# Third layer's low-rank factor kept in SBUF, adapters picked on TensorE, a bias folded into the weights, and the passage to the third layer reordered

## The reference, cut to what matters

```python
# dense 1: a weight masked in 32 x 32 blocks
out = x @ (W0 * block_mask).T
# dense 2: a weight, a bias, and one adapter of rank 16 chosen for each batch
y = x @ W1.T + bias
seg = searchsorted(starts, arange(B), side='right') - 1
adapter = clip(seg - 1, 0, 2)            # three adapters
y += where(seg > 0, (x @ A[adapter].T) @ B[adapter].T, 0)
# the attention-like layer: 1024 -> 128, four sub-layers (scan over tokens, MLP), 128 -> 1024
h = x @ Win.T + bin
for l in range(4):
    h = h + sconv(silu(layernorm(h) * ln1_w + ln1_b)) * sc_lin
    h = h + mlp(layernorm(h) * ln2_w + ln2_b)
out = (layernorm(h) * lnl_w + lnl_b) @ Wout.T + bout
# dense 3: a weight, a bias and eight experts of rank 16, mixed for each batch by a router
q = x[:, 179:-1].mean(axis=1)
routing = softmax(q @ router_W.T + router_b)
out = x @ W.T + b + 2 * sum_e routing_e * (x @ A_e.T) @ B_e.T
```

## Time and profile before

| | |
|---|---|
| median of 3 runs | 1789.1 us (1788.26 to 1795.86) |
| the profiled execution | 1785.82 us, span 1784.1 us, mean granted clock 0.978 |
| PE / weight loads | 1707.3 us (96%) / 1373.2 us (77%) |
| DVE / ACT / POOL | 1068.6 us (60%) / 654.7 us (37%) / 441.0 us (25%) |
| DMA | 199.76 MB, 112 GB/s; queues q1 and q10 (hardware dynamic), q8 and q14 (instructions) |
| dense 1, about | 0 to 375 us |
| dense 2, about | 375 to 880 us |
| MLP turns, about | 880 to 1244 us |
| passage and first pair | 1244 to 1320 us |
| dense 3, about | 1320 to 1784 us |

### The profile page before, as it was taken

How to read it: one execution, slowest core, us unless ns; L and a number is a source line. 1 busy time by engine, 2 the same in 40 slices (tenths; PEclk the granted TensorE clock), 3 DMA queues, 4 the chain that set the end, 5 groups by cost and what they waited for, 6 DMA issues and landing times.

```text
span 1784.1 us, 23303 instructions
## 1 busy us (share of the span) xinstructions
PE 1707.3 (96%) x8154; PEld 1373.2 (77%) x8154; DVE 1068.6 (60%) x2045; ACT 654.7 (37%) x967; POOL 441.0 (25%) x380
## 2 busy tenths in 40 slices
PE   6999999999999999999799999999699899999998
PEld 5788888888888888888666676666578688787886
DVE  6433443445555555566667777778567676776633
ACT  2433333333333333322334555545333333433321
POOL 4011111100000000000466777763122221211200
PEclk9999999999999999999889999999799999999999
DMA  6323333333323333333040000003445555555321
GB/s 249 107 94 119 115 122 121 122 112 116 112 102 114 109 108 110 109 114 107 39 151 24 1 1 1 1 15 124 155 131 213 162 191 186 178 181 183 126 94 60
DMA packets 81541, 199.76 MB, mean 112 GB/s; under 512 B 9746, under 2 KB 26130, under 8 KB 81170
## 3 DMA queue, kind: packets, MB, share of 16 engines
q1 hardware_dynamic: 60690, 129.07, 21.8%
q10 hardware_dynamic: 20736, 69.22, 9.7%
HBM read 125.89 MB, written 72.35 MB: 111 GB/s over the span
## 4 chain that ended last, share of the span: by engine, by line
PE 88%; DVE 4%; issue 4%; ACT 2%; POOL 1%; DMA 1%; ACTq 0%; SPq 0%; POOLq 0%; DVEq 0%
PE ps L666 19%; PE ps L668 18%; PE ps L667 18%; PE ps L843 6%; PE ps L788 3%; PE ps L680 3%; PE ps L725 2%; PE ps L794 2%; PE ps L834 2%; PE ps L835 2%; PE ps L833 2%; PE ps L727 2%; PE ps L726 2%; PE ps L749 1%; PE ps L811 1%
## 5 line engine op out<-in xcount | busy, mean ns | idle before, releaser
L666 PE MATMUL ps<-wall_x,x_hi 128*128 128x512 f32 x1008 | 399.8, 397 | 7.7 <-DVE wall_x L1328 3.7
L668 PE MATMUL ps<-wall_x,x_lo 128*128 128x512 f32 x1008 | 395.0, 392 | 0.0
L667 PE MATMUL ps<-wall_x,x_hi 128*128 128x512 f32 x1008 | 394.8, 392 | 0.0
L1926 POOL TENSOR_TENSOR rstd<-var_eps,minus_half 128x1 f32<-128x1 f32 x96 | 78.0, 812 | 925.1 <-DVE minus_mean L1363 917.9
L1354 DVE BATCH_NORM_STATS2 stats<-row 128x6 f32<-128x512 f32 x192 | 133.0, 694 | 183.1 <-ACT row L1038 178.8
L666 PEld LDWEIGHTS ps<-wall_x,x_hi 128*128 128x128 f32 x1008 | 190.6, 189 | 50.7 <-issue 10.3
L668 PEld LDWEIGHTS ps<-wall_x,x_lo 128*128 128x128 f32 x1008 | 190.6, 189 | 40.8
L667 PEld LDWEIGHTS ps<-wall_x,x_hi 128*128 128x128 f32 x1008 | 190.9, 189 | 37.9
L666 PE MATMUL ps<-wall_y,x_hi 128*128 128x512 f32 x512 | 202.8, 396 | 0.0
L668 PE MATMUL ps<-wall_y,x_lo 128*128 128x512 f32 x512 | 200.1, 391 | 0.0
L667 PE MATMUL ps<-wall_y,x_hi 128*128 128x512 f32 x512 | 199.7, 390 | 0.0
(11 more groups left out here) (243 smaller groups left out, 2935.9 us busy)
## 6 DMA issues: line engine op xcount, KB each, us to landing
x_scratch<-row ACTq DMA_DIRECT2D x64, 512.0 KB, 2.9
x_in<-x_scratch SPq DMA_DIRECT2D x64, 512.0 KB, 3.6
w_in<-in_w_t SPq DMA_DIRECT2D x96, 256.0 KB, 2.9
out<-row ACTq DMA_DIRECT2D x32, 512.0 KB, 2.6
x_in<-in_x_t SPq DMA_DIRECT2D x29, 512.0 KB, 3.4
cx<-x_scratch SPq DMA_DIRECT2D x24, 512.0 KB, 3.9
x_scratch<-cx ACTq DMA_DIRECT2D x24, 512.0 KB, 2.7
w_more<-in_w_t SPq DMA_DIRECT2D x32, 256.0 KB, 3.0
```

What stands on the lines that cost most here:

```text
L666: pe.matmul(bank, hi[:, k], wall[:, k, 0, cols], start=(k == 0), stop=False)
L667: pe.matmul(bank, hi[:, k], wall[:, k, 1, cols], start=False, stop=False)
L668: return pe.matmul(bank, lo[:, k], wall[:, k, 0, cols], start=False, stop=(k == KC - 1))
L1926: pool.tensor_tensor(rstd[:, i:i + 1], var_eps[:, i:i + 1], minus_half[:, 0:1], ALU.pow)\
```

## The change

1. Dense 2. The factors of all adapters are loaded once, 64 rows twice (the second copy in partitions 64 to 127), and `lora_hi` and `lora_low` make of them one fp32r matrix with the high parts in the first 64 rows and the low parts, with a sign, in the others. `choose(b)` scales a placement matrix by `coef`, and PE picks with it: `pick_b` gives the batch's B (2 matmuls of 512 columns), `pick_a` the chunk of A (1 matmul of 128 columns for every two parts); ACT copies both from PSUM (`take_b`, `take_a`). High and low parts lie in different rows of one operand, so a part is one matmul in place of three.
2. Dense 3. `expert_a` is loaded and split once, in dense 1, and stays in SBUF (`a_hi`, `a_lo`, 8 KB for each partition). The room comes from the descriptor reserve, 16 KB before and 1 KB now (`dynamic_dma_scratch_size=1024`, `CONST`).
3. The bias of the read-out. z is taken plus one (`one`, the bias of `silu_x`), the bias row over 128 is added to every row of `wout`, and the fourth matmul, `brow`, `ones`, `two_ones` and `bias_low` go.
4. The passage. The loop ends at turn 37; what was left is written out in another order. `rstd1` and `var1` are double, and units 38 and 39 have their own banks (`s1_bank`). LAG is 6.
5. Semaphores of the statistics are folded into `dve_done`.

```diff
-LAG = 4
+LAG = 6
-TURNS = LAST_END + 1
+TURNS = MLP_END + 6
...
-    CONST = 16512
+    CONST = 1152
...
     def weight_part(n):
...
-                pe.wait_ge(a_hi_ready, n // 2 + 1)
-                pe.wait_ge(a_lo_ready, n // 2 + 1)
+                if n < BATCHES * PARTS:
+                    pe.wait_ge(a_rows_ready, n // 2 + 1)
                 if n % PARTS == 0:
                     pe.wait_ge(b_hi_ready, 2 * b + 2)
-                    pe.wait_ge(b_lo_ready, 2 * b + 2)
+                bank = ps[:, part_bank(n)]
                 if n < BATCHES * PARTS:
                     at_least(pe, w_summed, n)
+                    pe.matmul(bank, a_rows[:, i], b_rows[:, cols], start=True, stop=True).then_inc(w_product, 1)
+                    return
...
+            def pick_b(b, half):
+                if half == 0:
+                    pe.wait_ge(pick_ready, b + 1)
+                    pe.wait_ge(lora_ready, 2)
+                    at_least(pe, w_summed, PARTS * b)
                 else:
+                    pe.wait_ge(b_hi_ready, 2 * b + 1)
+                pe.matmul(ps[:, 4], pick[:, 1], lora[:, 1, half * HALF:(half + 1) * HALF], start=True, stop=True)\
+                  .then_inc(b_picked, 1)
+
+            def pick_a(chunk):
+                k, i = chunk % KC, chunk % 2
+                at_least(pe, a_rows_ready, chunk - 1)
+                at_least(pe, h_evacuated, (chunk - KC - 2) // 2)
+                pe.matmul(ps[:, 7, HALF // 2 + P * i:HALF // 2 + P * (i + 1)], pick[:, 0], lora[:, 0, k * P:(k + 1) * P],
+                          start=True, stop=True).then_inc(a_picked, 1)
...
-                    pe.matmul(bank, lo, wout_hi[:, cols], start=False, stop=False)
-                    pe.matmul(bank, ones_rows[:], brow[:, cols], start=False, stop=True).then_inc(c_mm, 1)
+                    pe.matmul(bank, lo, wout_hi[:, cols], start=False, stop=True).then_inc(c_mm, 1)
...
             for s in range(A_END, B_END):
                 b, j, i = batch_of(s), s % TPB, s - A_END
+                if b + 1 < BATCHES and j == 0:
+                    pick_b(b + 1, 0)
+                if b + 1 < BATCHES:
+                    pick_a(KC * (b + 1) + j)
                 if s + 1 < B_END:
                     turn_x(s + 1)
-                product(s, 0)
+                if b + 1 < BATCHES and j == 0:
+                    product(s, 0, range(KC // 2))
+                    pick_b(b + 1, 1)
+                    product(s, 0, range(KC // 2, KC))
+                else:
+                    product(s, 0)
...
-                if turn == 37:
-                    turn_x(B_END)
-                if turn == 38:
-                    read_out(TPB)
-                if turn == 39:
-                    reduce_total(0)
+            turn_x(B_END)
+            spread_rstd1(LAST_END - 3)
+            variance1(LAST_END - 2)
+            variance1(LAST_END - 1)
+            read_out(TPB)
+            spread_rstd1(LAST_END - 2)
+            spread_rstd1(LAST_END - 1)
+            reduce_total(0)
             router_logits(0)
+            router_turn(0)
             read_out(TPB + 1)
-            router_turn(0)
...
# ACT, passage
+            square1(LAST_END - 2)
+            normalise_c(TPB - 2)
+            square1(LAST_END - 1)
+            silu_x(LAST_END - 3)
+            normalise_c(TPB - 1)
+            split_x(B_END)
+            silu_x(LAST_END - 2)
             router_exp(0)
             split_b(BATCHES)
-            normalise_c(TPB)
...
+                    silu_x(LAST_END - 1)
+                    build_parts(n, range(2))
                     split_x(p + 1)
-                    build_parts(n, range(PARTS))
+                    build_parts(n, range(2, 4))
+                    normalise_c(c)
+                    build_parts(n, range(4, PARTS))
...
# DVE, start of the MLP and passage
                     scale_wout()
-                    two_ones()
                 if turn == EARLY + 6:
-                    bias_low()
                     wout_low()
...
+            take_var1(LAST_END - 2)
+            take_var1(LAST_END - 1)
+            add_up(TPB - 2, 0)
+            scale1(LAST_END - 3)
+            add_up(TPB - 1, 0)
+            add_up(TPB - 1, 1)
+            scale1(LAST_END - 2)
+            split_x(B_END)
+            take_q(0)
+            residual_half(TPB, 0)
             router_first(0)
-            split_a(BATCHES * PARTS // 2)
             router_second(0)
+            residual_half(TPB, 1)
             take_coef(0)
+            residual_end(TPB)
             split_b(BATCHES)
...
+                    scale1(LAST_END - 1)
+                    build_parts(n, range(2))
                     split_x(p + 1)
-                    build_parts(n, range(2))
-                    residual(c + 1)
-                    build_parts(n, range(2, PARTS))
+                    build_parts(n, range(2, 3))
+                    residual_half(c + 1, 0)
+                    build_parts(n, range(3, 4))
+                    residual_half(c + 1, 1)
+                    residual_end(c + 1)
+                    build_parts(n, range(4, PARTS))
...
# SP, passage
-            for m in range(3, UNITS):
+            for m in range(3, UNITS - 2):
                 store_z(m)
             load_x(B_END + 1)
+            for i in range(2, 4):
+                load_w(BATCHES * PARTS + i)
+            for m in range(UNITS - 2, UNITS):
+                store_z(m)
...
# POOL, turns and passage
+                for c in first_tiles(turn - 1)[1:]:
+                    root_c(c)
                 for c in first_tiles(turn - 2):
                     add_up(c)
-                for c in first_tiles(turn - 1)[1:]:
-                    root_c(c)
-                if turn == 39:
-                    root_c(TPB)
+            root1(LAST_END - 2)
+            root1(LAST_END - 1)
+            add_up(TPB - 2)
+            root_c(TPB)
```

More of the change, by code:

```diff
@@ new lines, in weight_part @@
+                    return
+                if n % PARTS == 0:
+                    pe.wait_ge(a_lo_ready, 1)
+                    pe.wait_ge(b_lo_ready, 2 * (b - BATCHES) + 2)
+                pe.wait_ge(w_summed, n - 1)
+                rows = slice(k * P, (k + 1) * P)
+                pe.matmul(bank, a_hi[:, rows], b_hi[:, cols], start=True, stop=False)
+                pe.matmul(bank, a_hi[:, rows], b_lo[:, cols], start=False, stop=False)
+                pe.matmul(bank, a_lo[:, rows], b_hi[:, cols], start=False, stop=True).then_inc(w_product, 1)
@@ L915, in _ @@
                     turn_x(A_END)
+                if s >= PARTS and s % 2 == 0:
+                    pick_a((s - PARTS) // 2)
                 product(s, 0)
+                if s == PARTS - 1:
+                    pick_b(0, 0)
                 if s >= PARTS:
@@ L1415, in adapter_coef @@
                 dve.wait_ge(small_loaded, 7 * 16)
-                dve.wait_ge(adapter_parts, 2)
-                after(dve.memset(coef[:], 0.0))
+                dve.wait_ge(ident_ready, 1)
+                for i, first in enumerate((0, LOW)):
+                    rows = ident[:, first:first + ADAPTERS * RANK]
+                    mark(dve.tensor_reduce(group[:, i], rows.rearrange("p (a j) -> p a j", j=RANK), AX, ALU.add))
                 for b in range(BATCHES):
-                    after(dve.tensor_scalar(below[:, b], starts[:], float(b), None, ALU.is_le))
+                    mark(dve.tensor_scalar(below[:, b], starts[:], float(b), None, ALU.is_le))
@@ L1420, in adapter_coef @@
+                settle()
+                mark(dve.tensor_tensor(group[:, 0], group[:, 0], group[:, 1], ALU.add))
                 after(dve.tensor_reduce(count[:], below[:], AX, ALU.add))
[L1421 to L1423 removed]
+                for i in range(ADAPTERS):
+                    mark(dve.tensor_scalar(chosen[:, i], count[:], float(i + 2), None, ALU.is_equal))
@@ new lines, in adapter_coef, with pick_places @@
+                settle()
+                after(dve.tensor_scalar(coef[:, 0:BATCHES], chosen[:, 0], group[:, 0, 0:1], None, ALU.mult))
+                for i in range(1, ADAPTERS):
+                    after(dve.scalar_tensor_tensor(coef[:, 0:BATCHES], chosen[:, i], group[:, 0, i:i + 1],
+                                                   coef[:, 0:BATCHES], ALU.mult, ALU.add))
+            def pick_places():
+                mark(dve.memset(low_row[:], 0.0))
+                after(dve.memset(place[:], 0.0))
+                mark(dve.memset(low_row[LOW:], 1.0))
+                for i in range(2):
+                    for g, first in enumerate(((0, 0, LOW), (0, LOW, 0))[i]):
+                        rows = ident[:, first:first + ADAPTERS * RANK]
+                        mark(dve.tensor_reduce(place[:, i, RANK * g:RANK * (g + 1)],
+                                               rows.rearrange("p (a j) -> p j a", j=RANK), AX, ALU.add))
+                settle()
+                after(dve.tensor_scalar(row_sign[:], low_row[:], -2.0, 1.0, ALU.mult, ALU.add))
@@ L1425, in take_biases, with choose, lora_low @@
```

(7 more changed lines are left out.)

307 lines of the change are left out of this document (157 added, 150 removed).

## The result

The changed kernel took 1727.61 us (median of 4 runs, 1726.88 to 1728.08); the kernel before took 1788.68 us beside it. The ratio is 0.965, with a 95% interval of 0.9624 to 0.9675: 61 us faster. The forecast was 1720 us, the range 1704 to 1741. The sum of the terms was 67.5 us; the two profiled executions differ by 58.4 us (1784.1 and 1725.7 us of span), less than the medians, since that of the kernel before (1785.82 us) was 2.9 us under its median.

A forecast was written before the change was run, and what follows sets the result against it. TensorE (PE), busy 96% of the span, was taken as the bound. Terms of 23.0, 12.7, 3.5, 10.7 and 17.6 us sum to 67.5, giving 1718.3 from the profiled execution and 1721.6 from the median; forecast 1720 us, range 1704 to 1741.

The forecast's parts named there:

- A: Dense 2 weight parts: one matmul instead of three, less the picks, plus waits gone at batch starts; net gain 23.0 us.
- I take 0.2: Dense 2: assumed PE time in us for each of 32 pick_a matmuls, 6.4 us in all, because a lone matmul pipelines badly.
- The lower end: Dense 2: pick_a's cost from below, by 256-column starts 0.12 us apart and 128-column transposes at 0.109 us; total 3.5 us.
- Rival 1: Dense 2: picks stall PE, which waits for ACT's copies; 1803 us at 2.6 us more per tile; chance 2%.
- B: Read-out in MLP turns and dense 3: bias matmul folded away, 60 x 0.2267 = 13.6 us, less tile 7's four: 12.7 us.
- C: Start of the MLP: bias_low and other bias work go, so PE's wait for z and half the half-clock loss go; 3.5 us.
- What bounds: Opening section: TensorE busy 96% of the span; a removed wait of another engine counts only if PE stood behind it.
- Rival 3: Dense 3 read-out tiles: DVE becomes the bound and the 44 folded matmuls give nothing; 1730 us; chance 8%.
- D: Passage from the MLP to dense 3: new order brings the first parts sooner; gain 10.7 us, four bias matmuls included.
- Rival 2: Passage stays as long as it was, first parts at half clock, only four matmuls gained; 1730 us; chance 15%.
- E: Dense 3 weight builds: resident A removes first-part waits and half clock for second to fourth batch (6.0, 4.8, 6.8); 17.6 us.

The follow-up runs named there:

- first experiment: Changed kernel with GpSimd's order in the MLP turns undone, its two add_up again before the root of the odd tile: 1724.07 us, 3.5 us less.

## Why the prediction came out as it did

The sum was 67.5 us and the executions gave 58.4; what was off, step by step:

- **A** (23.0, measured 26.8). The 29.0 us for the matmuls stand (30.5 when put back). The step that failed is "I take 0.2" for pick_a: 32 x 0.07 = 2.2 us, not 6.4, 4.2 us less, which accounts for the difference of 3.8. The lower end was made from the right rows; the argument that a lone matmul between two kinds pipelines badly is what the runs refute. The Trainium skill's 81 ns (TensorE: Matmul & The Clock Gate, "Back-to-back issue gap") lies near the lone pick's 0.07 us and under the 0.112 us of the further ones. Rival 1 never showed: PE waited for no pick.
- **A low clock at tile 60** (-1.5, no term). It is under "The hardware" below.
- **B in the MLP and C** (6.2, measured 0.5). I priced the folded matmuls at full PE and VectorE's work by its durations in the kernel before. GpSimd's new order was followed only in the passage, and I never asked what it would run beside. The step that failed is that VectorE's operations were taken at a fixed duration: GpSimd over VectorE took back 3.3 us (first experiment), and wout_lo takes 2.32 us over GpSimd's rotation. Another 0.9 us went at the start of the MLP (27.3 us at half clock from 851.42 on, 23.9 before). That is not the change: the unaltered kernel has 23.9 us there in its second trace, and does not lose them. With C's 0.7 us below, 0.8 us of the 5.7 are left, less than the 1.5 us of the folded matmuls that the test with the fourth matmul finds hidden. C was forecast at 3.5 us; 2.8 of it shows between the two kernels, in the turn where bias_low stood, and put back it costs 5.3, of which 3.0 in the profiled execution is in the passage.
- **B in dense 3** (10.0, measured 5.6). "What bounds": the cover checked was VectorE, and it held, 11.95 us of 14.49. What became late was x_in, and PE's load of x was priced at no wait without a look at its queue: SyncE's was read for the passage only. Rival 3 named the right tiles and the wrong engine; 4.4 of its 10 us came true, 2.9 of them by SyncE's order.
- **D** (10.7, measured 10.1). PE's timeline in the passage after, against the earlier trace rows:

```profile
1228.51 1.92 PE L921 MATMUL ps<-token_weight,total 128*128 128x1 f32 x16 [1.53 <-DVE total L1811]
1231.71 0.55 PE L928 MATMUL ps<-rw,q 128*1 128x8 f32 x16 [1.28 <-DVE q L1819]
1234.64 0.26 PE L933 MATMUL ps<-ident,wide 1*128 1x1 f32 x1 [2.39 <-DVE wide L1832]
1238.52 0.76 PE L743 MATMUL ps<-b_hi,a_hi 128*128 128x512 f32 x1 [0.76 <-DVE b_lo L1457]
```

  From turn_x(B_END) to the first part it is 20.0 us; the prediction had 20.1 (27.2 before). From there to the pair's end it is 45.0; the prediction had 44.5. The chain laid out for VectorE came true step by step: coef ends 17.5 us after turn_x(B_END) (17.6 in the prediction), b_lo 19.8 (20.0), and weight sum 4 ends 14.7 us after the first part (14.7). That the size is right owes a little to errors that cancel: LAG 6 cost 1.4 us against the 1 us allowed for a low clock, and the steps named from the low part at 1280.6 on add up to about 1307.1, not 1307.7. Half clock lasted 17.06 us in the two stretches shown next, but they end before weight sum 2 (1246.34), while PE was behind VectorE's chain; that they cost nearly nothing is read from the timelines and was not run. Of these 10.1 us, resident factors alone give 2.1. What each move in the order gives was not run.

```profile
1223.47:1226.88 3.41, 3.02 (x11) 1.73 (x9) 1.85 (x4) 2.15 (x3) 3.41 (x3) 0.50 0.00 0
1230.30:1243.95 13.65, 9.22 (x42) 7.05 (x42) 10.45 (x26) 4.28 (x8) 0.56 (x1) 0.50 0.45 158
```

  Rival 2 was right that half clock stays, and wrong that the length stays: the first parts do run at half clock, but the chain ahead of them is VectorE's and not PE's.
- **E** (17.6, measured 17.2, and 17.2 alone). 4.9, 5.3 and 6.9 us stand against 6.0, 4.8 and 6.8. The clock followed the wait: no idle ahead of the first part, no half clock in these tiles.

## What to carry to other kernels

When a tile on the bound engine gets shorter, check every queue that feeds it at the new length, the DMA issuer's before the vector engine's: the next wait here was a load that stood in order behind another one's wait. When an order is changed on GpSimd or VectorE, lay the two timelines side by side: here a VectorE operation with both inputs in SBUF ended only after the GpSimd operation that it met, and one taken out of VectorE's list handed its wait on to the next. Before a difference of a microsecond is given a cause, read a second trace of the same kernel: here one stage differed by 0.8 us with nothing changed. Price a matmul that a trace lacks from the start-to-start distance of the same number of columns, not from a guess about changes of kind.

## What the runs showed of the hardware

- VectorE and GpSimd. The two sums of each engine in the MLP of the changed kernel, one instruction to a line:

```profile
1206.83 1.28 POOL L2110 TENSOR_TENSOR total<-c_first,total 128x512 f32<-128x512 f32 x1
1206.87 1.79 DVE L1814 TENSOR_TENSOR total<-c_first,total 128x512 f32<-128x512 f32 x1
1208.26 1.54 POOL L2110 TENSOR_TENSOR total<-c_first,total 128x512 f32<-128x512 f32 x1
1208.77 1.58 DVE L1814 TENSOR_TENSOR total<-c_first,total 128x512 f32<-128x512 f32 x1
```

  VectorE's sum takes 0.69 us where GpSimd does not read beside it. Here each ends 0.55 us after GpSimd's (1208.66 after 1208.11, 1210.35 after 1209.80), and GpSimd's second, which starts inside VectorE's first, takes 1.54 us and not 1.28. wout_lo (1.22 us alone) ends 1.08 us after the rotation's end at 934.83, and bias_low in the kernel before 1.08 us after its end at 959.22. In the changed kernel's trace all 31 of VectorE's sums and differences of 512 columns with both inputs in SBUF that start during a 512-column operation of GpSimd end 0.55 to 0.58 us after it. Operations with an input in PSUM keep 0.68 us. So the later one waits until the other has ended, for all but 0.14 us of itself, and the lost time is what is left of the other's operation. The Trainium skill ("SBUF — State Buffer", section "Who interferes with whom") says that a VectorE instruction with two SBUF inputs contends with a GpSimd instruction that reads SBUF, calls the shared ports an exclusive lock and has the order of issue decide who blocks. These rows agree: one after the other, the four would take 1.28 + 0.69 + 1.27 + 0.69 = 3.93 us, and with 0.14 us less at each of the three changes 3.51; they took 3.52.
- The clock can fall with no idle time ahead of it. At tile 60 the changed kernel has this stretch, 0.9 us after 32 matmuls of one column, with PE busy all the time:

```profile
761.57 3.62 PE L814 MATMUL ps<-vec,w 128*128 128x1 f32 x32
```

```profile
766.09:769.50 3.41, 3.41 (x10) 2.64 (x9) 2.17 (x3) 1.54 (x2) 0.32 (x1) 0.50 0.19 73
```

  The kernel before and the one with the parts three times run the same 32 matmuls in 3.6 us and stay at full clock. With five picks the stretch is 6.82 us; with only the resident factors added to the kernel before it is 3.41 us again. Since that kernel's dense 2 is the one of the kernel before, and the kernel before has one trace, the -1.5 us cannot be put down to the change. What decides was not found; 3.41 us at half clock are worth 1.6 us here.
